# A decoder layer on one core: in the causal attention cores GpSimd adds the probabilities of the key tiles, with three score banks and one value bank

## What is computed

```python
x = x + attn(layernorm(x))                       # causal, 16 heads of 32
x = x + xattn(layernorm(x), ctx, pos)            # cross attention, 32 heads of 16, no mask
x = x + ffn_block(layernorm(x))                  # inside: causal attention with rotary, then experts

# each causal attention, per batch item and head
scores = where(causal, q @ k.T * scale, NEG)     # 512 x 512
out    = softmax(scores) @ v                     # then all heads @ w_out
```

## Time and profile before

| | |
|---|---|
| median of 3 runs | 2362.08 us (2354.91 to 2368.24) |
| the profiled execution | 2356.96 us, its span 2355.2 us |
| mean granted TensorE clock | 0.948 of full speed |
| PE, DVE, ACT, POOL busy over the span | 91%, 55%, 38%, 18% |
| first causal core, 170 to 465 us: PE, DVE, ACT, POOL busy | 284.20, 167.53, 133.69, 20.43 of 295 us |
| rotary causal core, 1280 to 1575 us | 283.54, 167.36, 133.54, 20.42 of 295 us |
| cross core, 630 to 1100 us | 422.99, 386.36, 305.20, 60.67 of 470 us |
| experts, 1575 to 2355 us | 731.02, 218.76, 150.60, 124.64 of 780 us |

### The profile page before, as it was taken

The page is one execution under the profiler, slowest core; times in us unless marked ns, Lnnn a source line. Parts: engine busy times, 40 slices in busy tenths (PEclk is TensorE's granted clock), DMA queues, the critical chain, the costliest instruction groups (busy, mean ns, idle before and its releaser), DMA issues.

```text
span 2355.2 us, 32522 instructions
## 1 busy us (share of the span) xinstructions
PE 2139.2 (91%) x11159; PEld 1378.0 (59%) x11159; DVE 1286.2 (55%) x2847; ACT 900.4 (38%) x1694; POOL 417.9 (18%) x320
## 2 busy tenths in 40 slices
PE   6999999977689999996988999988999998999998
PEld 5775656656333333333766566556888877666564
DVE  5546665477779898985886655634332142222221
ACT  3334444343357676764333544424322220111111
POOL 0000000046501111111554000001000000133332
PEclk9997999989779999998997999998999998999999
DMA  5556565255643545434457655435021043333331
GB/s 183 184 191 142 124 150 135 79 184 217 252 121 86 129 110 128 116 96 130 162 197 237 144 117 133 118 99 209 19 90 45 27 164 118 130 59 62 65 63 35
DMA packets 138806, 297.21 MB, mean 126 GB/s; under 512 B 24914, under 2 KB 27092, under 8 KB 137620
## 3 DMA queue, kind: packets, MB, share of 16 engines
q1 hardware_dynamic: 115508, 243.74, 35.0%
q10 hardware_dynamic: 14400, 32.77, 4.6%
q0 software_dynamic: 8736, 18.62, 4.1%
HBM read 181.55 MB, written 102.50 MB: 121 GB/s over the span
## 4 chain that ended last, share of the span: by engine, by line
PE 41%; issue 18%; DVE 9%; DMA 5%; POOL 3%; ACT 1%; SPq 1%; POOLq 0%; DVEq 0%; ACTq 0%
PE bank L1460 10%; PE bank L1548 8%; PE bank L1471 4%; PE bank L1567 4%; PE bank L429 3%; PE bank L934 3%; PE bank L988 2%; POOL cross_c_attn_parts L1234 2%; PE bank L965 2%; PE bank L1006 2%; DMA qk_parts<-cross_p_parts 1%; DMA normed<-xt 1%; DMA stack<-rotary_c_max_rows 1%; PE bank L1532 1%; POOL cross_c_xt L1224 1%
## 5 line engine op out<-in xcount | busy, mean ns | idle before, releaser
L1101 ACT ACTIVATE cross_c_prob<-bank 128x512 f32<-128x512 f32 x512 | 270.6, 597 | 135.6 <-PE bank L965 134.5
L1133 DVE TENSOR_REDUCE cross_c_row_max<-bank 128x2 f32<-128x1024 f32 x256 | 300.1, 1211 | 33.6 <-PE bank L934 27.1
L934 PE MATMUL bank<-stack 48*128 48x512 f32 (+4 forms) x768 | 240.1, 486 | 44.4 <-PEq L70 19.5
L1460 PE MATMUL bank<-moe_hT,moe_w 128*128 128x512 f32 x1056 | 260.2, 404 | 2.2 <-DVE moe_hT L1702 2.2
L965 PE MATMUL bank<-stack 56*128 56x512 f32 (+4 forms) x768 | 233.9, 403 | 22.7 <-ACT cross_c_prob L1101 10.8
L934 PEld LDWEIGHTS bank<-stack 48*128 48x128 f32 (+1 forms) x768 | 105.4, 202 | 239.9 <-DVE cross_c_row_max L1133 105.6
L1460 PEld LDWEIGHTS bank<-moe_hT,moe_w 128*128 128x128 f32 x1056 | 205.7, 196 | 46.9 <-DVE moe_hT L1702 2.6
L1548 PE MATMUL bank<-moe_w_e,moe_hT_e 128*128 x624 | 194.4, 465 | 2.2 <-DMA moe_w_e<-in_experts_packed 1.7
L1129 DVE CUSTOM_DVE_ANT_0 first_c_masked<-bank,later 128x128 f32<-128x128 f32 (+3 forms) x256 | 119.3, 487 | 97.0 <-PE bank L934 96.0
L1129 DVE CUSTOM_DVE_ANT_0 rotary_c_masked<-bank,later 128x128 f32<-128x128 f32 (+3 forms) x256 | 119.2, 487 | 90.3 <-PE bank L934 86.3
L1101 ACT ACTIVATE first_c_prob<-bank 128x512 f32<-128x512 f32 (+3 forms) x256 | 108.7, 436 | 151.0 <-PE bank L968 148.6
(11 more groups left out here) (336 smaller groups left out, 3805.5 us busy)
## 6 DMA issues: line engine op xcount, KB each, us to landing
stack<-qk_parts SPq DMA_DIRECT2D x96, 256.0 KB, 5.9
stack<-qk_parts SPq DMA_DIRECT2D x384, 64.0 KB, 2.4
moe_w_e<-in_experts_packed SPq DMA_DIRECT2D x8, 2176.0 KB, 8.5
qk_parts<-first_p_parts SPq DMA_DIRECT2D x32, 512.0 KB, 2.7
qk_parts<-cross_p_parts SPq DMA_DIRECT2D x32, 512.0 KB, 2.8
qk_parts<-rotary_p_parts SPq DMA_DIRECT2D x32, 512.0 KB, 2.7
moe_raw<-in_shared_packed SPq DMA_DIRECT2D x11, 768.0 KB, 11.5
xt<-x SPq DMA_DIRECT2D x8, 1024.0 KB, 6.0
```

Source lines behind the costliest of these rows:

```text
L934: last = nc.tensor.matmul(bank[:, 0 : width_q(m)], q_stack[slot][r : r + PRODUCT_ROWS, at, m * P : (m + 1) * P], k_stack[slot][r : r + PRO ...
L1101: nc.scalar.activation(prob[:, n % PROB_SLOTS, 0 : S - q0], psum[bank_at["score", n]][:, 0 : S - q0], ACT.Exp).then_inc(s.exp_done, 1)
L1133: nc.vector.tensor_reduce(row_max[:, g % 2, m, j - 1 : j + 1], c.banks[:, first : first + WIDE, :], AX_X, ALU.max).then_inc(s.max_done, 1)
L1460: last = nc.tensor.matmul(psum[bank][:], weights(pa, f, k), hT[p % 2][:, pb, k, :], start=m == 0, stop=m == len(steps) - 1)
```

## The change

In the causal cores:

- each key tile has its own buffer `prob0` to `prob3` of four heads in place of the eight slots. GpSimd adds them (`add_keys`): `total` = `prob0` (its queries from 128 on) + `prob1`, then + `prob2`, then + `prob3`, each add over the queries that the later tile has. The first 128 queries see key tile 0 alone;
- of the ones sets two per group are left (`sums`): one of 128 columns from `prob0` at step 9 right behind the value set, and one of 384 columns from `total` at step 4 of the next group, which waits for `added`;
- value sets stand at step 4m + 9 (`VALUES_LAG`), in one value bank, so the first of a group waits for `attn_out` of the group before; the freed bank is a third score bank;
- VectorE turns the sums at step 5 as before, takes the reciprocal and turns it back at step 6, and multiplies at step 7 in a `scale` of its own, which stands behind `split_max`;
- `max_transpose` and `take_max` move from step 9 to 8, `attn_high` from 8 to 10, the projection's thirds from (1, 2, 3) and (13, 14, 15) to (6, 7, 10) and (12, 14, 15);
- the values are loaded per group (256 KB) in three slots, not per batch item (1 MB) in two.

```diff
-        MAX_STEP = 9
-        FLIP_STEP, NORM_STEP = (4, 8) if cross else (5, 5)
+        MAX_STEP = 9 if cross else 8
+        FLIP_STEP, NORM_STEP = (4, 8) if cross else (5, 6)
...
-                  [[(1 + m // 2, step) for step in ((13, 14, 15) if m % 2 else (1, 2, 3))] for m in range(TT)])
+                  [[(1 + m // 2, step) for step in ((12, 14, 15) if m % 2 else (6, 7, 10))] for m in range(TT)])
...
+        VALUES_LAG, SUMS_STEP = 7 if cross else 9, 4
+        bank_score, bank_shared = ((0, 1, 2, 3), (4, 5, 7)) if cross else ((0, 1, 4), (2, 3, 7))
+        bank_o, bank_sum = (6, 6) if cross else (5, 6)
...
+                    def sums(g, first):
+
+                        if first:
+                            pe.wait_ge(s.exp_done, g * N16 + HEADS_AT_ONCE)
+                            if g:
+                                pe.wait_ge(s.flip, g)
+                        else:
+                            pe.wait_ge(s.added, (TT - 1) * (g + 1))
                         for j in range(HEADS_AT_ONCE):
...
+                            out = psum[bank_sum][32 * j : 32 * j + 32]
+                            if first:
+                                last = nc.tensor.matmul(out[:, 0:P], c.ones[:], prob_of[0][:, j, 0:P], start=True, stop=True)
+                            else:
+                                last = nc.tensor.matmul(out[:, P:S], c.ones[:], total[:, j, :], start=True, stop=True)
+                        last.then_inc(s.sums_done, 1)
...
+                            if causal and step % HEADS_AT_ONCE == 0 and g:
+
+                                act.wait_ge(s.pv_done, n // HEADS_AT_ONCE - TT + 1)
+                                act.wait_ge(s.added, (TT - 1) * (g - 1) + max(1, step // HEADS_AT_ONCE))
+                                if step == 0:
+                                    act.wait_ge(s.sums_done, 2 * g - 1)
...
+                            if causal and step == 6 and g + V_SLOTS - 1 < GROUPS:
+                                load_values(act, g + V_SLOTS - 1)
...
+                            if step == NORM_STEP + 1 and g and causal:
+                                scale(g - 1)
...
+                    def add_keys(g, m):
+
+                        pool.wait_ge(s.exp_done, g * N16 + (m + 1) * HEADS_AT_ONCE)
+                        if m == 1:
+                            if g:
+                                pool.wait_ge(s.sums_done, 2 * g)
+                            first = prob_of[0][:, :, P:S]
+                        else:
+                            pool.wait_ge(s.added, (TT - 1) * g + m - 1)
+                            first = total[:, :, (m - 1) * P :]
+                        nc.gpsimd.tensor_tensor(total[:, :, (m - 1) * P :], first, prob_of[m][:], ALU.add).then_inc(s.added, 1)
...
                     for g in range(GROUPS):
...
+                        for m in range(1, TT if causal else 0):
+                            add_keys(g, m)
+                            if g and m == (TT - 1 if g + 1 < GROUPS else 1):
+                                attn_low(g - 1)
```

134 lines of the change are left out of this document (78 added, 56 removed).

## The result

The changed kernel took **2387.13 us** (median of seven, 2381.74 to 2390.52) against 2363.01 us for the kernel before in the same comparison: a ratio of 1.009, with a 95% interval of 1.0062 to 1.0118. It is slower, by 0.9%. The profiled execution has a span of 2380.0 us at a mean granted clock of 0.923; before it was 2355.2 us at 0.948. The two profiled executions, taken apart at the last VectorE instruction of each core: the first causal core ends 13.2 us later (484.7 us for 471.5), and from the end of the cross core to the end of the rotary core pass 496.6 us for 480.7, 15.8 more. Of the rest, what lies between the first core's end and the cross core's takes 626.5 us for 624.8, and what follows the rotary core 772.3 for 778.1; the change does not touch either, so differences of that size are between one execution and another.

What follows compares the result with a forecast made beforehand. TensorE's own instruction list was taken as the bound; group savings less group 1 and tail costs gave -21 us per causal core, -42 in all, from 2357 to 2315, 2320 us as a median; range 2292 to 2380.

Steps and rivals of the forecast that it cites:

- the first rival: GpSimd's first add shuts VectorE out in `split_max`, 3.8 us per plain group: 2388 us as a median, slower; chance 0.17.
- Ones sets, removed: TensorE in the causal cores gives up 1.9 us per group, 61 us over 32 groups.
- The sum, -42 us: Nine plain groups at -1.5, six with projections at -2.1, +2, +4, -1: -21 us per core, two cores -42.
- the 0.75 us at the transposes: TensorE waits some 0.75 us at step 8 for `split_max` in plain groups; projection thirds cover it in the others.
- The timeline behind the ones set: Times from s, start of the instruction behind step 4's 384-column set: flip s + 0.14, L1141 s + 2.5, L1143 s + 2.7.
- a tie within my error: In plain groups GpSimd's first add starts at s + 2.65 to 2.75, L1143 at s + 2.7; forecast favoured VectorE.
- third rival: More TensorE waits for row maxima go, 1.2 us per group instead of 0.3, and the 0.75 is covered: 2300 us; chance 0.17.
- Second rival: The tie falls differently from group to group, half the plain groups blocked: 2354 us, no change; chance 0.14.
- GpSimd's adds, 3.84 + 2.56 + 1.28: GpSimd's three adds per group, in proportion to elements: 7.7 us as upper bound unless VectorE blocks; skill-based estimate 7.1.
- the fourth rival: Sums come late: slow adds of 9.7 us make the 384-column set wait about 1.2 us in plain groups: 2345 us; chance 0.07.
- Group 1, +2 per core: VectorE's two-SBUF-operand L1208 at steps 11 and 14 meets GpSimd's adds: +1 to 3 us, taken as 2 per core.
- the tail, +4 per core: At each causal core's end, GpSimd's adds, `attn_low` and the last ones set follow the last exponential: +4 us per core.

Runs made afterwards that it cites:

- experiments 4 and 2: Changed kernel each: 4 with all ones sets back on TensorE, no GpSimd adds, 2359.31 us; 2 with GpSimd's first add waiting for `split_max`, 2342.68 us.
- experiment 5: Changed kernel with `split_max` ahead of `normalise` and the residual load moved from step 4 to step 12, in the causal cores: 2308.82 us.
- the control 9: The kernel before the change, with only the residual load moved from step 4 to step 12: 2349.76 us.
- experiment 7: Changed kernel with `split_max` ahead of `normalise` and both the residual and the value loads at step 12: 2308.67 us.
- experiment 1: Changed kernel with `split_max` moved ahead of `normalise` in step 6 of the causal cores: 2336.64 us.
- experiment 10: Changed kernel with only the residual load moved to step 12, `split_max` still behind `normalise`: 2386.07 us.
- experiments 6: Changed kernel with `split_max` ahead of `normalise` and the value loads moved from step 6 to 12, residual load at step 4: 2336.3 us.
- experiment 12: On top of experiment 7: output weights' low halves at steps 0, 3, 13, 14 of group 1, last group's `attn_low` behind the third add: 2315.64 us.

## Why the prediction was wrong

The forecast was 2320 us, faster; the time fell on the first rival's, 2388 us, by its mechanism, and outside my range. Point by point:

- **Ones sets, removed, -1.9 us per group: right.** The like pair is experiments 4 and 2, whose plain groups take 14.64 and 12.56 us: 2.1 us, 0.3 of which are a shorter wait for `split_max` (0.83 and 0.53 us), so 1.8 for the sets. The three groups with the projections that follow take 54.4 us (262.09 to 316.50) and 48.4 (253.82 to 302.24), 2.0 each.
- **The sum, -42 us: reached once both interferences are gone.** Experiment 5 against the control 9, the same place of the residual load in both: 2308.8 - 2349.8 = -41 us. Its four groups from 300.87 to 362.65 take 61.8 us, the control's 69.4, so -7.6, where two plain and two with projections were to give 2 x (-1.5) + 2 x (-2.1) = -7.2. The agreement to 1 us is better than that of the terms: an undisturbed plain group gains 1.8 us (12.6 for 14.4) and not 1.5, one that waits for the max rows 1.0. And experiment 5 is not the kernel that I forecast: with `split_max` early the 0.75 us at the transposes are gone, and TensorE waits 0.63 to 0.67 us at the first value set of plain groups instead, for an exponential. The rows of experiment 5:

```profile
300.87 0.60 PE L968 MATMUL bank<-ident,first_c_max_parts 128*8 128x128 f32 x4
314.28 0.60 PE L968 MATMUL bank<-ident,first_c_max_parts 128*8 128x128 f32 x4
328.62 0.60 PE L968 MATMUL bank<-ident,first_c_max_parts 128*8 128x128 f32 x4
346.56 0.60 PE L968 MATMUL bank<-ident,first_c_max_parts 128*8 128x128 f32 x4
362.65 0.60 PE L968 MATMUL bank<-ident,first_c_max_parts 128*8 128x128 f32 x4
```

```profile
302.42 1.06 PE L1017 MATMUL bank<-first_c_prob,first_c_v 128*32 128x512 f32 x8 [0.66 <-ACT first_c_prob L1139]
```

- **The timeline behind the ones set: right to 0.03 us.** In the changed kernel's group shown above s is 388.68. The flip came at s + 0.14 (forecast the same), L1141, now L1181, at s + 2.52 (2.5), L1143, now L1183, at s + 2.69 (2.7), the add at s + 2.67 (2.65 to 2.75).
- **The step that failed: "a tie within my error", taken for VectorE.** The argument was that "GpSimd wants its operands some 0.1 us behind its reported start". It does not give VectorE these 0.1 us. In the 13 groups that were blocked the add started 0.02 to 0.03 us ahead of L1183; where it started 0.17 us or more behind it (0.19 at least in experiment 5, 0.17 in 7), L1183 took 0.17 to 0.18 us. A lead of 0.02 us in the reported starts is already enough. From 0 to 0.17 us in VectorE's favour no run has a row. Nothing in the trace of before could show on which side of zero the 0.02 us would fall, and so the two cases deserved about even chances, not 0.45 (with the third rival's 0.17) against 0.17. What the failed step cost is 50 us as the kernel stands (experiment 1) and 77 us once the residual load is out of the way (experiment 10 against 5); it is why the time came out slower.
- **Second rival, a tie that falls differently from group to group: wrong.** The order repeats to 0.01 us in every steady group of a kind: -0.02 or -0.03 us in plain groups, 0.88 to 0.92 with projections. Behind the first three groups only one plain group (maxima at 234.68 us) had VectorE ahead, by 0.55 us. With a schedule this regular, a tie is decided once for all groups.
- **The rival's price: near by luck, since errors cancel.** It had 3.8 us per plain group for eighteen groups and no clock. But the last group of a core has no `split_max`, so sixteen could be blocked at most, and the adds were shorter than assumed, 3.44 us. In the profiled execution 13 L1183s and two L1181s were held: 15 waits of 3.6 to 3.8 us, 56 us. Missing was the clock. Experiment 10, with 16 such waits (60 us), against 5 puts the whole at 2386.1 - 2308.8 = 77 us, although 5 has some 10 us of other waits in the same groups. That the 17 to 27 us left are the half clock behind the waits fits the records, in which TensorE's clock stands at half for 157 us of the two causal cores of experiment 10 and for 58 us in experiment 5; no run separates the two.
- **GpSimd's adds, 3.84 + 2.56 + 1.28: the upper bound, as said.** They took

```profile
L1291 POOL TENSOR_TENSOR first_c_total<-first_c_prob 128x1536 f32<-128x1536 f32 x16 | 55.1, 3442 | 262.7 <-ACT first_c_prob L1139 262.7
L1291 POOL TENSOR_TENSOR first_c_total<-first_c_total,first_c_prob 128x1024 f32<-128x1024 f32 x16 | 38.1, 2379 | 54.6 <-ACT first_c_prob L1139 54.6
...
L1291 POOL TENSOR_TENSOR first_c_total<-first_c_total,first_c_prob 128x512 f32<-128x512 f32 x16 | 20.5, 1282 | 16.3 <-ACT first_c_prob L1139 15.0
```

  7.1 us together (groups of GpSimd's instructions of the changed kernel in the first core: total, mean in ns). The estimate from the Trainium skill (GPSIMD Engine Reference, Elementwise), 7.1 us, was the better one. They held the 384-column set only in the last group of each core, so the fourth rival did not come.
- **Group 1, +2 per core, and the tail, +4 per core: of that size by the waits.** One L1263 of 2.43 us made TensorE wait 2.22 us; in the last group it waited 3.1 us for the adds. The experiments to win these back failed for other reasons.
- **Not in the sum: the residual load.** I costed the value loads at nothing, which experiments 6 and 7 bear out, and left the residual load out without a reason: I did not ask which transfer would run into the max rows once the groups were shorter. In the changed kernel it did not show, since the blocked groups were long enough (experiment 10). The price appears only when the first interference is gone: 28 us. It would have spoilt the forecast by itself: with no block, but with this load, the change gives 2337 to 2343 us (experiments 1 and 2), not 2320.

Of the lock itself the Trainium skill (SBUF — State Buffer, Who interferes with whom) says that a VectorE instruction with two SBUF inputs and a GpSimd instruction that reads SBUF exclude each other for their whole length, and that the one issued first wins. All runs here agree: 16 elements waited 3.42 us, and the swap and the held-back add gave the time back. Where one of VectorE's two inputs was in PSUM it did not wait: in experiment 5 `scale` at 376.83 and a masked maximum at 377.44, both inside an add that began at 376.47, took their usual 0.69 and 0.28 us. L1181, whose only tensor input is in SBUF, did wait, 2.92 us; it is a `tensor_scalar`, like L577 in the earlier trace rows. I had quoted this rule and then argued a tie against it.

## What to carry to other kernels

When work is moved to GpSimd, list VectorE's instructions on the critical path that have two SBUF inputs or are of L1181's kind (`tensor_scalar`), however small, and put them in front of GpSimd's long instruction with a margin, by order or by a wait; where your own timeline calls it a tie, count the loss at even chances, or make the margin part of the change. After a change that shortens a loop, look up again which transfer leaves just ahead of the small one that everybody waits for: its cover was the time that you took away. And when you price a wait of TensorE, add what its clock may lose behind it.

## What was not expected of the hardware

- The order between a VectorE and a GpSimd instruction with reported starts 0.02 to 0.03 us apart decides over 3.4 us, and it fell the same way in nearly every plain group: 13 times in the changed kernel, 14 in experiment 10.
- With the 13 waits of 3.8 us for L1183 the records show TensorE at its lower level, 1.2 GHz, nine times for 6.8 us and four times for 3.4: 1.94 us for the value set instead of 1.06. A shorter wait may or may not cost this: 2.22 us in experiment 7 (until 217.65) was followed by a stretch at 0.50, the same wait in experiment 5 (2.23 us, until 219.59) by 1.00, and 1.49 us in experiment 12 again by 0.50. That lets runs of one kernel differ. The windows of both, 220 to 225 us, experiment 7 first:

```profile
220.00:225.00 5.00, 5.00 (x22) 3.07 (x19) 2.71 (x9) 1.68 (x3) 1.41 (x2) 0.50 1.05 226
```

```profile
220.00:225.00 5.00, 5.00 (x37) 3.22 (x35) 4.73 (x16) 2.98 (x6) 2.75 (x2) 1.00 0.76 164
```

- 64 KB issued behind 2.8 MB landed some 8 us later with all DMA engines full, though the larger loads were issued by other instructions, 1.25 MB of them on ScalarE's queue. The Trainium skill (DMA: Bandwidth & Descriptors, Issuing engines are not separate DMA queues) says that transfers of all issuing engines interleave on the same 16 DMA engines; the trace agrees, with a busy share of 1.01 to 1.13 from 300 to 320 us.
